# Attention values in another order: both query halves of a key tile behind each other, one copy per unit instead of two

## The reference, cut to what matters

```python
B, N, D, H = 4, 1024, 256, 16          # DK = D // H = 16
qkv = (x @ w_qkv).reshape(b, n, 3, H, DK)
q, k, v = (qkv[:, :, i].transpose(0, 2, 1, 3) for i in range(3))
attn = jnp.einsum('bhnd,bhmd->bhnm', q, k) * (1.0 / np.sqrt(DK))
attn = jax.nn.softmax(attn, axis=-1)
y = jnp.einsum('bhnm,bhmd->bhnd', attn, v)
```

## Time and profile before

| | us |
|---|---|
| median of 3 runs | 1542.8 |
| the runs | 1540.32, 1542.8, 1558.97 |
| the profiled execution | 1542.8 |
| its span, first to last instruction | 1541.0 |
| attention, first scores to last copy | 520.2 to 1175.8 of the span |

### The profile page before, as it was taken

The page is one execution under the profiler, slowest core; times in us unless marked ns, Lnnn a source line. Parts: engine busy times, 40 slices in busy tenths (PEclk is TensorE's granted clock), DMA queues, the critical chain, the costliest instruction groups (busy, mean ns, idle before and its releaser), DMA issues. The chain is left out here.

```text
span 1541.0 us, 32155 instructions
## 1 busy us (share of the span) xinstructions
PE 1448.0 (94%) x11962; PEld 899.2 (58%) x11962; DVE 1266.3 (82%) x2433; ACT 1019.7 (66%) x1737; POOL 370.2 (24%) x633
## 2 busy tenths in 40 slices
PE   8688989997999999999999999999998769999997
PEld 7455656565655344444444444444445559999996
DVE  6899999964567689999999999999964867777773
ACT  3699999963433478888888888888886522222221
POOL 3011111103111012222222222222222732222222
PEclk9799999999999789999999999999999979999999
DMA  3300101014875724334444443344342765656561
GB/s 116 96 8 15 47 23 46 15 63 170 270 269 183 175 63 97 93 97 100 98 94 88 97 92 92 83 91 90 81 133 59 255 249 195 214 195 220 193 215 49
DMA packets 147307, 186.04 MB, mean 121 GB/s; under 512 B 68288, under 2 KB 99008, under 8 KB 147152
## 3 DMA queue, kind: packets, MB, share of 16 engines
q1 hardware_dynamic: 126896, 157.27, 35.1%
q0 software_dynamic: 19280, 26.46, 5.6%
q10 hardware_dynamic: 976, 0.24, 0.1%
HBM read 129.67 MB, written 54.21 MB: 119 GB/s over the span
## 5 line engine op out<-in xcount | busy, mean ns | idle before, releaser
L1700 ACT ACTIVATE at_p<-at_pst 128x512 f32<-128x512 f32 x1024 | 555.6, 597 | 85.8 <-PE at_pst L1750 70.4
L1714 DVE TENSOR_REDUCE at_mx<-at_pmx 128x2 f32<-128x1024 f32 x488 | 578.7, 1216 | 17.9 <-PE at_pmx L1741 12.5
L1762 PE MATMUL at_pacc<-at_p,at_v 128*32 128x256 f32 x4096 | 332.6, 397 | 0.4 <-ACT at_p L1700 0.2
L1741 PE MATMUL at_pmx<-at_k,at_q 48*128 48x512 f32 x976 | 248.0, 504 | 2.2 <-PEq L1218 1.1
L1750 PE MATMUL at_pst<-at_q,at_k 50*128 50x512 f32 x1024 | 218.5, 410 | 0.3 <-ACT at_p L1700 0.3
L1741 PEld LDWEIGHTS at_pmx<-at_k,at_q 48*128 48x128 f32 x976 | 92.1, 185 | 209.6 <-issue 144.2
L878 PE MATMUL ws_pA<-ident,ws_A 128*128 128x128 f32 x1088 | 150.4, 284 | 24.5 <-ACT ws_A L660 22.1
L878 PEld LDWEIGHTS ws_pA<-ident,ws_A 128*128 128x128 f32 x1088 | 120.4, 144 | 84.4 <-ACT ws_A L660 39.1
L1750 PEld LDWEIGHTS at_pst<-at_q,at_k 50*128 50x128 f32 x1024 | 157.0, 188 | 12.8 <-ACT at_p L1700 6.3
L1762 PEld LDWEIGHTS at_pacc<-at_p,at_v 128*32 128x32 f32 x4096 | 81.2, 108 | 136.1 <-ACT at_p L1700 80.5
L2267 DVE STREAM_TRANSPOSE ex_zr<-ex_row 32x64 f32<-32x64 f32 x608 | 143.3, 236 | 15.7 <-DMA ex_row<-scratch_routed 7.8
(11 more groups left out here) (271 smaller groups left out, 1612.8 us busy)
## 6 DMA issues: line engine op xcount, KB each, us to landing
ex_w<-in_L_ffn_w SPq DMA_DIRECT2D x39, 1024.0 KB, 5.6
at_q<-scratch_qs SPq DMA_DIRECT2D x192, 64.0 KB, 3.2
at_k<-scratch_ks SPq DMA_DIRECT2D x192, 64.0 KB, 3.3
ex_row<-scratch_routed SPq DMA_DIRECT2D x39, 258.0 KB, 5.1
scratch_qs<-gp_split SPq DMA_DIRECT2D x16, 512.0 KB, 3.8
scratch_ks<-gp_split SPq DMA_DIRECT2D x16, 512.0 KB, 4.1
scratch_v<-gp_v SPq DMA_DIRECT2D x8, 1024.0 KB, 6.0
at_v<-scratch_v SPq DMA_DIRECT2D x32, 256.0 KB, 3.7
```

The lines of the kernel that those rows point to most:

```text
L1700: a.activation(pt[:, n % BUFS, k % 2, :], pst[(w * 2 * STEPS + k) % BANKS][:], ACT.Exp).then_inc(exped, 1)
L1714: v.reduce_max(mx[w % 2][:].rearrange("p (h n) k -> p h n k", h=2)[:, :, j // 2, j % 2], pmx[n % SLOTS][:], AX.X).then_inc(taken, 1)
L1741: last = nc.tensor.matmul(pmx[n % SLOTS][:, h, :], att.rows(qst[u], h, ROWS)[:, nt * P:(nt + 1) * P], att.rows(kst[u], h, ROWS)[:, kh * HA ...
L1762: last = nc.tensor.matmul(pacc[at:at + 2 * DK, p * QUARTER:(p + 1) * QUARTER], vst[u][:, t, h, :], pt[:, n % BUFS, h, c * QUARTER:(c + 1) ...
```

## The change

The steps of a unit are taken in another order: `t = s // 2` and `p = s % 2`, so the two halves of the queries follow each other on one key tile. Both halves of the bank `pacc` are open during the whole unit. The first step's V is left out; the second step's V does the work of both, with matmuls of 512 columns over two adjoining buffers of `pt` and `start=True` for the whole bank, and counts `pv` twice. The later V blocks have 256 columns, as before. `pacc` is complete only at the end of a unit: it is copied in one piece of 512 columns, behind the exponential k = 4 of the next unit (`COPY`), and the first V of a unit, now in step 3 of the issue order instead of step 2, waits for that copy. `oed` counts one for each unit, and `fold` waits accordingly.

```diff
     def fold(self, sp, w):
-        sp.wait_ge(self.oed, 2 * (w + 1))
+        sp.wait_ge(self.oed, w + 1)
...
-    COPIES = 18, 2
+    COPY = 4
...
-            def out(w, p):
-                a.wait_ge(pv, w * STEPS + (p + 1) * BT)
-                if p == 0 and w >= 2:
+            def out(w):
+                a.wait_ge(pv, (w + 1) * STEPS)
+                if w >= 2:
                     a.wait_ge(outputs.y_out[w % 2], w // 2 * outputs.MOVES)
-                at = p * QUARTER
-                a.copy(oe[w % 2][:, at:at + QUARTER], pacc[:, at:at + QUARTER]).then_inc(oed, 1)
+                a.copy(oe[w % 2][:], pacc[:]).then_inc(oed, 1)
...
-                    if k == COPIES[0]:
-                        out(w, 0)
-                    if k == COPIES[1] and w:
-                        out(w - 1, 1)
-            out(UNITS - 1, 1)
+                    if k == COPY and w:
+                        out(w - 1)
+            out(UNITS - 1)
...
             def scores(n, h):
-                u, p, t = w % RING, s // BT, s % BT
+                u, t, p = w % RING, s // 2, s % 2
...
             def values(n):
                 w, s = n // STEPS, n % STEPS
-                u, p, t = w % RING, s // BT, s % BT
+                u, t, p = w % RING, s // 2, s % 2
+                if s == 0:
+                    return
+                first = 0 if s == 1 else p
                 pe.wait_ge(exped, 2 * n + 2)
-                if n and t == 0:
-                    pe.wait_ge(oed, 2 * w + p)
+                if s == 1 and w:
+                    pe.wait_ge(oed, w)
                 for h in range(2):
                     for c in range(2):
                         at = (2 * h + c) * 2 * DK
-                        last = nc.tensor.matmul(pacc[at:at + 2 * DK, p * QUARTER:(p + 1) * QUARTER], vst[u][:, t, h, :],
-                                                pt[:, n % BUFS, h, c * QUARTER:(c + 1) * QUARTER], start=(t == 0), stop=(t == BT - 1))
-                last.then_inc(pv, 1)
+                        out = pacc[at:at + 2 * DK, first * QUARTER:(p + 1) * QUARTER].rearrange("d (p j) -> d p j", j=QUARTER)
+                        last = nc.tensor.matmul(out, vst[u][:, t, h, :], pt[:, n % BUFS - p + first:n % BUFS + 1, h, c * QUARTER:(c + 1) * QUARTER],
+                                                start=(s == 1), stop=(s == STEPS - 1))
+                last.then_inc(pv, 2 if s == 1 else 1)
```

## The result

| | before | changed |
|---|---|---|
| median, us | 1542.13 (20 runs) | 1553.44 (20 runs) |
| lowest to highest | 1535.02 to 1558.97 | 1547.11 to 1562.55 |
| span of the profiled execution | 1541.0 | 1543.0 |

The ratio is 1.0081, with a 95% interval of 1.006 to 1.0101: the changed kernel is slower by 12.5 us, between 9.3 and 15.6. Forecast were 1560 us, 17.8 more than before, and a range of 1548 to 1572.

What follows compares the result with a forecast made beforehand. TensorE's serial block stream, about 20.0 us a unit, was taken as the bound. Units 1 to 30 at 0.60 each (18.0), unit 31 +0.25, last copy +0.21, unit 0 -0.3, last steps -0.4: +17.8 on 1542.8, said 1560, range 1548 to 1572.

Steps and rivals of the forecast that it cites:

- ScalarE's saved copies: One ScalarE copy of two goes, 0.16 us less work a unit; worth nothing in steady state.
- the start of a unit: Steps 2 to 4 of a unit: M of step 4 comes at 2.80 instead of 2.20, 0.60 us later, not won back.
- The merge: On TensorE, two V blocks become one of 1.01 us, saving a fixed part of 0.13 us a unit.
- the rule that the prediction weighed: Skill's warm matmul time, N/2.4 + 2.5 ns: merging V would save about 0.01 us, total some 1564 us; not adopted.
- the hold by the wide copy: Step 3's merged V waits for the copy ending at 1.64 and starts at 1.79; 0.60 us a unit, chance 0.72.
- the bank tie: Scores k = 7 of step 3 need the bank of k = 4, so TensorE waits until that exponential ends at 1.10.
- the rival on the other side: No hold at the unit's start if the copy ends before about 1.0: only gains remain, 1536.6 us; chance 0.08.
- the sign that was to tell: Step 3's V starts 1.79 behind the scores of step 2; a start at 1.5 or before would refute the forecast.
- the -0.4 for the last 24 steps: In the last 24 steps, without M, ScalarE's saved 0.27 at a step-9 copy may count twice: between 0 and -0.6.
- Unit 0: The first unit has no copy to wait for and saves a fixed part: -0.3 us, between 0 and -0.5.
- The fold: Rival: the later copy makes fold's transfer late and stalls VectorE, 15 us more, 1575 us; chance 0.07.
- The clock in unit 0: Rival: unit 0's low-clock stretch ends earlier (1549.6 us, chance 0.07) or lasts another unit (1575 us, chance 0.06).

Runs made afterwards that it cites:

- e1: The changed kernel with the accumulator copy cut to 8 of 512 columns: 20.36 us a unit, 1549.5 us against 1541.6 before, ratio 1.0047.
- e5: e1 with exponential k = 4 of each unit but the first cut to 64 of 512 columns: 19.99 us a unit, 1536.3 us against 1543.5 before.
- e2: The changed kernel with the wide copy two exponentials earlier (COPY = 2): 20.65 us a unit, 1560.5 us, ratio 1.0144 to before.
- e10: The changed kernel again, unaltered, for a second profile: unit 0 of 28.5 us, units 1 to 29 in 595.7 us, median unit 20.50 us.
- e7: The kernel before with eight extra 512-column matmuls in steps 0 and 1 of unit 0: 1542.5 us, ratio 0.9991, unit 0 of 33.4 us.

## Why the prediction was right, and where it was off

*What bounds.* Right. TensorE's serial stream set 20.0 us a unit, the hole in it moved everything, and VectorE idled 0.70 before a reduction and caught up without a cost. ScalarE's saved copies were worth nothing that shows: the start of a unit costs 0.52 and the whole unit 0.50. No run tests them by themselves.

*The places on the time scale.* Forecast and measured behind the scores of step 2: copy 1.05 and 1.00; its end 1.64 and 1.58; V 1.79 and 1.72; merged V 1.01 and 1.00; M 2.80 and 2.72. Of the 0.07 of V, 0.05 come from the first term. I took 0.55 from an exponential to the copy behind it out of the earlier trace rows, where the copy had to wait for V as well, whose row ends at 793.67 + 0.64 = 794.31. Without such a wait it is 793.63 - 793.13 = 0.50. The start of a unit was priced at +0.60, came to +0.52, and 0.50 is what a whole unit shows. The merge saves 0.13 to 0.14 against two blocks of 0.57, as the rows had it, and not the 0.01 of the rule that the prediction weighed. By that rule (the Trainium skill, TensorE: Matmul & The Clock Gate, Back-to-back issue gap) the merged V would have taken 1.13, an estimate; it took 1.00.

*The name of the loss.* Here the step was right in size and half wrong in reason. I called it the hold by the wide copy. e1 takes the copy away and keeps 0.36 of the 0.52. e5 loosens the bank tie too, and nothing of the 0.36 is left. I had both waits on the time scale, at 1.10 and at 1.79, but charged the sum to the later one. This matters for the rival on the other side: I wrote that the gains would be left if the copy ended before 1.0. In e1 it ended at 810.73 + 0.16 = 810.89, that is 1.15, 0.41 ahead of V, so it held V no longer, and the kernel still stood 8 us above before. In e2 it ended at 0.39, well before 1.0, and a unit took 20.65. In e5 it ended at 812.26 + 0.16 - 811.65 = 0.77, and a unit took 19.99, not the 19.8 of that rival. What decides is when the exponential k = 4 ends. That V starts later than 1.5, the sign that was to tell, holds in e1 as well (1.56): it does not tell the copy from the tie.

*The sum.* Units 1 to 29 cost 597.16 - 581.43 = 15.7 in the first two profiles. Over all profiles the means are 596.4 for the changed kernel and 581.7 for before, so 14.7; forecast were 17.4 for these 29. That is the term which was mis-sized, by 2.7 us. Unit 30, which has no M in its second half, lost 0.2 and not 0.60; unit 31 with its last copy lost 0.45, and forecast were 0.25 + 0.21. With the -0.4 for the last 24 steps the ends were forecast at 0.7 and came to 0.6. Unit 0 was priced at -0.3; the profiles give -2, where two profiles of one kernel differ by 6. So the sum is 14.7 + 0.6 - 2 = 13 us. The measured interval of 9.3 to 15.6 holds both this and the 15 without unit 0, so the time does not tell between them.

*The rivals.* The fold did not come late in most units: VectorE waited for its transfer twice, 1.2 us in all, and in e10 not once in this window. Read to the letter, such a wait was to be a sign of being wrong, but the kernel before shows one as well (0.4 to 0.8 us). The working had it land at 8.1, where its terms give 4.1 + 3.7 = 7.8. The clock in unit 0 does what was feared: unit 0 takes 25.0 to 31.3 us in the kernel before and 22.5 to 28.5 in the changed one. That is 6 us within either kernel, and the stretch behind the attention adds up to 12 more. Both are part of the spread of single executions. How much of either is in the difference of the medians isn't shown.

## What to carry to other kernels

Leaving a block out of an in-order stream helps only if the next block may start earlier. See what ties it before you count the saving: here three score banks made the spared 0.57 us a pause, the work came back later as one long block, and the start of a unit came 0.36 us later than before even without a wait for the copy. When a copy and a bank both hold an engine in the same place, price each of them with the other one gone. And compare stretches rather than spans where single executions differ by more than the effect: 29 units agree within 0.5 us between the profiles of before, the spans of the same three only within 13 (1541.0, 1538.0, 1528.4).

## What the runs showed of the hardware that I had not expected

- A second half of the scores that starts alone is followed by V after 0.42 us (e1: 811.30 - 810.88), a pair after 0.34.
- A V that waits for ScalarE's copy starts 0.15 behind its end in the earlier trace rows; in the changed kernel 794.35 - (793.63 + 0.58) = 0.14.
- TensorE was busy without a gap from 522 to 550 in the first profile of before, and was granted the lower level, 1.2 GHz, for nearly all of it (0.51). With eight more matmuls at the start (e7) the mean there was 0.51 too. What ends such a stretch stays open.
